# Second attention of a four-layer kernel: each score matmul one place later in TensorE's order, the fourth of a step behind the value products

## The reference, cut to what matters

```
def _L1_attn_ref(x, w_qkv, w_out, b_out):      # x: (4, 1024, 128), 16 heads of 8
    ...
    q, k = _apply_rope(q, cos_emb, sin_emb), _apply_rope(k, cos_emb, sin_emb)
    scores = jnp.einsum('bhqd,bhkd->bhqk', q, k) / jnp.sqrt(jnp.asarray(hd, x.dtype))
    attn = jax.nn.softmax(scores, axis=-1)
    out = jnp.einsum('bhqk,bhkd->bhqd', attn, v)
```

## Time and profile before

| what | value |
| --- | --- |
| median of 3 runs | 1924.15 us (1923.0 to 1927.66) |
| the profiled execution: its own time | 1922.64 us |
| its span, first to last instruction | 1920.8 us |
| PE / DVE / ACT busy over the span | 91% / 72% / 61% |
| second attention, first to last value product | 867.5 to 1565.9 us |

### The profile page before, as it was taken

The page is one execution under the profiler, slowest core; times in us unless marked ns, Lnnn a source line. Parts: engine busy times, 40 slices in busy tenths (PEclk is TensorE's granted clock), DMA queues, the critical chain, the costliest instruction groups (busy, mean ns, idle before and its releaser), DMA issues.

```text
span 1920.8 us, 31169 instructions
## 1 busy us (share of the span) xinstructions
PE 1743.9 (91%) x9328; PEld 844.8 (44%) x9328; DVE 1389.2 (72%) x2540; ACT 1162.8 (61%) x1801; POOL 97.0 (5%) x123
## 2 busy tenths in 40 slices
PE   6899999699999999579999999999999968988997
PEld 3334343366656656333333333333333325544553
DVE  3788888757777777478889888989898814455544
ACT  3888888544344444107777777777777754444443
POOL 1000000001111011010000000000000000011000
PEclk9899999889999999859999999999999988999999
DMA  7532121101111000210000000000100010000000
GB/s 220 140 92 60 49 62 47 66 1 34 33 33 33 29 10 28 66 41 22 22 23 21 22 21 21 22 22 21 37 26 21 2 44 1 6 6 11 5 5 11
DMA packets 44844, 68.99 MB, mean 36 GB/s; under 512 B 15952, under 2 KB 25056, under 8 KB 44144
## 3 DMA queue, kind: packets, MB, share of 16 engines
q1 hardware_dynamic: 44784, 68.28, 11.9%
HBM read 42.04 MB, written 26.21 MB: 36 GB/s over the span
## 4 chain that ended last, share of the span: by engine, by line
PE 70%; DVE 12%; ACT 9%; issue 5%; SPq 1%; DMA 1%; POOL 1%; DVEq 1%; ACTq 0%; POOLq 0%
PE full_o L689 13%; PE score L676 12%; PE hid_pair L960 11%; PE bank L1060 9%; ACT probs L738 6%; PE causal_o L451 5%; PE triple L435 4%; PE max_pair L652 3%; DVE cprobs L514 2%; PE bank L969 2%; PE bank L990 2%; DVE hid L1317 1%; PE bank L890 1%; PE max_pair L663 1%; DVE negmax L776 1%
## 5 line engine op out<-in xcount | busy, mean ns | idle before, releaser
L776 DVE TENSOR_REDUCE negmax<-max_pair 128x1 f32<-128x1024 f32 x512 | 599.9, 1218 | 69.4 <-PE max_pair L652 62.3
L738 ACT ACTIVATE probs<-score 128x512 f32<-128x512 f32 x1024 | 529.0, 603 | 150.8 <-PE score L676 150.8
L652 PE MATMUL max_pair<-k_st,q_st 64*128 64x512 f32 x1024 | 405.3, 474 | 22.2 <-DMA q_st<-q_scr 18.1
L676 PE MATMUL score<-q_st,k_st 64*128 64x512 f32 x1024 | 382.9, 451 | 34.0 <-ACT probs L738 24.6
L676 PEld LDWEIGHTS score<-q_st,k_st 64*128 64x128 f32 x1024 | 170.6, 185 | 304.7 <-ACT probs L738 284.9
L484 ACT ACTIVATE cprobs<-triple 128x1536 f32<-128x1536 f32 x192 | 268.5, 1456 | 38.5 <-PE triple L435 38.3
L689 PE MATMUL full_o<-probs,v_st 128*32 128x512 f32 x2048 | 272.9, 606 | 0.0
L960 PE MATMUL hid_pair<-x_hi,w_hi 128*128 128x512 f32 x384 | 206.8, 539 | 0.0
L652 PEld LDWEIGHTS max_pair<-k_st,q_st 64*128 64x128 f32 x1024 | 171.7, 191 | 79.5 <-DVE negmax L776 39.5
L1132 ACT ACTIVATE act_s<-hid_pair 128x512 f32<-128x512 f32 x128 | 76.4, 597 | 157.5 <-PE hid_pair L960 157.4
L514 DVE TENSOR_SCALAR cprobs<-cprobs 128x1536 f32<-128x1536 f32 (+6 forms) x272 | 163.0, 624 | 0.4 <-ACT cprobs L484 0.4
(11 more groups left out here) (129 smaller groups left out, 1594.0 us busy)
## 6 DMA issues: line engine op xcount, KB each, us to landing
k_st<-k_scr SPq DMA_DIRECT2D x64, 128.0 KB, 2.8
q_st<-q_scr SPq DMA_DIRECT2D x128, 64.0 KB, 2.3
q_st<-q_scr SPq DMA_DIRECT2D x16, 512.0 KB
k_st<-k_scr SPq DMA_DIRECT2D x64, 104.0 KB
q_scr<-qk_hi SPq DMA_DIRECT2D x24, 256.0 KB, 2.9
k_scr<-qk_hi SPq DMA_DIRECT2D x24, 256.0 KB, 3.1
q_scr<-qk_lo SPq DMA_DIRECT2D x16, 256.0 KB, 2.9
k_scr<-qk_lo SPq DMA_DIRECT2D x16, 256.0 KB, 3.2
```

Of the source, the lines that this page charges most:

```text
L652: ins = nc.tensor.matmul(ring[slot][:, half, :], q_st[p][rows, qt * P:(qt + 1) * P], k_st[p][rows, j, half * CH:(half + 1) * CH], start=Tr ...
L676: nc.tensor.matmul(sbank[L.score_bank(e)][:, :], k_st[p][rows, j, kt * P:(kt + 1) * P], q_st[p][rows, q0:q0 + w], start=True, stop=True, t ...
L738: nc.scalar.activation(probs[s % NP][:, j, :], sbank[L.score_bank(e)][:, :], ACT.Exp, scale=SCALE).then_inc(L.exp_done, 1)
L776: nc.vector.tensor_reduce(negmax[:, qt // TPC, j, qt % TPC:qt % TPC + 1], ring[slot][:, :, :].rearrange("p a n -> p (a n)"), AXX, ALU.max, ...
```

## The change

In every step the scores are issued one place later. Place 0 now holds the fourth score that the step before issued at its place 3, so that it stands behind the value products; places 1 to 3 hold the first three scores of step s + 2. The order of the heads within a step becomes 0, 2, 3, 1, by which each place keeps the half of the array that it had. ScalarE's Exp writes the matching slice of `probs`. Ahead of the first round 7 scores are issued where there were 8. Gap, banks, counts to wait for, the halves of the maxima, the value products, and the order on ScalarE, VectorE, SyncE and GpSimd stay.

```
+    HEADS = (0, 2, 3, 1)
...
-            s, j = e // HG, e % HG
+            s, j = e // HG, L.HEADS[e % HG]
             qc, kt, q0, w, _ = L.steps[s]
-            if j == 0 and kt == 0:
+            if e % HG == 0 and kt == 0:
                 pe.wait_ge(L.aug_loaded[p][qc], 16 * 2 * (i // 2 + 1))
...
-                to = s + AHEAD
-                ahead = (i, p, to) if to < L.S else (i + 1, 1 - p, to - L.S) if nxt else None
                 pairs = L.pairs_at(s, nxt)
                 for j in range(HG):
-                    if ahead:
-                        pe_score(pe, L, ahead[0], ahead[1], HG * ahead[2] + j)
+                    e = HG * (s + AHEAD) + j - 1
+                    if e < L.E:
+                        pe_score(pe, L, i, p, e)
+                    elif nxt:
+                        pe_score(pe, L, i + 1, 1 - p, e - L.E)
...
-            for e in range(HG * AHEAD):
+            for e in range(HG * AHEAD - 1):
                 pe_score(pe, L, 0, 0, e)
...
-                nc.scalar.activation(probs[s % NP][:, j, :], sbank[L.score_bank(e)][:, :], ACT.Exp,
+                nc.scalar.activation(probs[s % NP][:, L.HEADS[j], :], sbank[L.score_bank(e)][:, :], ACT.Exp,
```

## The result

| | before | with the change |
| --- | --- | --- |
| median of 20 runs | 1919.85 us | 1927.47 us |
| ratio, 95% interval | | 1.0036 (1.0022 to 1.0049) |
| the profiled execution: its own time | 1922.64 us | 1932.16 us |
| its span | 1920.8 us | 1930.3 us |
| second attention, start of the first value product to start of the last | 697.8 us | 703.6 us |

By the ratio the change costs 6.9 us (4.2 to 9.4); the two medians themselves lie 7.6 apart. The forecast was +2.4 us, and its range, 1920 to 1932, held the time. Ratios here are of fast runs alone; the one run that this leaves out anywhere took 3805 us, one of ten of the version with half 0 first, and no profile shows why. The profile's 9.5 us is more than the change's share: the second attention accounts for 5.8 of them.

A forecast was written before the change was run, and what follows sets the result against it. A loop over TensorE and ScalarE, 2.61 us a step through three score banks, was taken as the bound. Terms +7.1 - 2.9 - 1.7 - 0.1 = +2.4 us on a median of 1924.15 gave 1926.6 us, range 1920 to 1932.

The forecast's parts named there:

- Interior step: Usual steps of the second attention: the loop of scores, Exps and value products stays at 2.61 us, a change of 0.
- The rival of a broken loop: Interior steps: place 3 no longer waits, steps fall towards VectorE's 2.35 us, about -60 us, near 1865; chance 0.05.
- Steps 8 and 0: Steps with the output save: ScalarE's copy leaves the loop, 0.10 us won in each of 29 steps, -2.9 us.
- Static rounds: Rounds 0 and 15: the Exp on the path has one wait fewer, 0.06 us less in 28 steps, -1.7 us.
- Steps 6 and 14: Left-out bank: place 2 stalls for the Exp of place 0, 0.23 us in each of 31 steps, +7.1 us.
- place 3 follows at once: Steps 6 and 14: score 34 starts 0.34 us behind the stalled place 2, value products another 0.32 later.
- upper bound of 0.34: Steps 6 and 14: cost per stall if value products follow the second pair by the full 0.43, 10.5 us in all.
- Start and tail: Before the first value products one score fewer, -0.5 us; at the end the last score comes later, +0.3 to +0.4.
- SyncE: Loads of the stacks of round i + 2 are issued 1.4 us later, covered by 8 us, so no cost.
- Within 0.3%: Whole-kernel time differing by less than 0.3% (5.8 us), about what a measurement can't tell from none; chance 0.71.
- slower: Whole kernel slower by over 0.3%: dear stall, half of the longer Exp and the forecast's upper edge; chance 0.21.
- The dear-stall rival: Steps 6 and 14 lose 0.34 us each and the save at steps 8 and 0 wins nothing, +8.8, 1933 us; chance 0.16.

The follow-up runs named there:

- the version with half 0 first: Changed kernel with half 0 of pair b's maxima issued ahead of the score at place 2 in steps 6 and 14; ratio 1.0019 to the kernel before.
- the copy put back: Changed kernel with the earlier turn, plus ScalarE's output copy again ahead of the Exp of place 0; 1918.44 us, ratio 0.9987 to the kernel before.
- the exchanged waits: Kernel before, with the two waits of a step's first Exp exchanged in static rounds 0 and 15 (score first, then value products); ratio 1.0005.
- the earlier turn: Changed kernel with the left-out bank turn one score earlier, ahead of scores 31 and 63; 1915.19 us, ratio 0.9974 to the kernel before.
- the first experiment: The changed kernel unaltered, measured and profiled again beside the kernel before on one chip; ratio 1.0033.

## Why the prediction was right, and where it was short

- **Interior step, 0.** Right: 2.61 in every step between the breaks. The loop runs over three banks, and renaming its members leaves it as it is. The rival of a broken loop is out.
- **Steps 8 and 0, -2.9.** Right: 2.67, forecast 2.68, against 2.78; the copy put back restores 2.78.
- **Static rounds, -1.7.** Right: 2.61, against 2.67; the exchanged waits give the same in the old order. The two static steps 8 had been put at nearly nothing and are 2.76 for 2.70, 0.1 us in all. One static step stands apart: step 14 of round 0 took 2.95 before, its Exp 0.88 behind place 0; with the change it is 2.84, and 2.61 with the earlier turn. Where its extra 0.28 came from is not shown; it lowers the difference of the profiles by as much and stands in no term of the sum.
- **Steps 6 and 14, +7.1.** The place and the stall were right; this is the term that was sized too small. The step was "place 3 follows at once", which took the half of the maxima at place 2 to start with its score. In the 28 looped cases it starts 0.08 later, so each costs 0.31 and not 0.23: 28 x 0.31 + 3 x 0.23 = 9.4, 2.2 more than forecast. My upper bound of 0.34 held it.
- **Start and tail.** 0.55 won at the start (from the first score to the first value product 7.91 us for 8.46), 0.56 lost at the end; forecast were -0.5 and +0.3 to +0.4.
- **SyncE.** Right: no wait of TensorE for the stacks appeared.
- **The sum.** With the corrected term it is +9.4 - 3.1 - 1.7 + 0 = +4.6. From first score to last value product the two profiles of the changed kernel show +5.3, of which 0.8 is the clock in step 1, and +4.4. The ratio's interval, 4.2 to 9.4 us, holds 4.6; its middle is 2 us higher. The runs of the first experiment narrow this down. Among runs of one kernel there (31 before, 12 with the change), a run is about 1.4 us longer for each 0.001 that its mean granted clock is lower, and the changed kernel's runs had 0.0005 less on average. At an equal clock the two kernels are 5.0 us apart there, an estimate with a standard error of 0.3. For the first comparison the clocks of the runs before are not on record, so its 2 us stay open.
- **The time.** That the forecast median of 1926.6 lies only 0.9 from the measured 1927.47 is luck. It stood on a median of 3 runs, 1924.15; over 20 runs the kernel before has 1919.85. Of the difference the forecast had 2.4 us where 6.9 were measured. Carried over as a difference, the range was -4 to +8, and it still holds the 6.9, near its upper end.
- **The side.** "Within 0.3%" had 0.71 and "slower" 0.21; the measured ratio lies just beyond 0.3%, with an interval on both sides of it. The dear-stall rival was nearer on one half (it had 0.34 a stall, the looped ones took 0.31) and wrong on the other (the save did win).

## What to carry to other kernels

A rotation of buffers that leaves out a turn, to come out even at a loop's end, is a part of the schedule: the two scores behind it wait for a more recent Exp than the others do, and here this was free only where the value products stood between them, or where the two scores used different rows of the array. Whoever moves the order by one place should look at the turn with it; here, on one chip, moving it turns +0.33% into -0.26%. And an operation outside the loop on the path, like the copy, was better placed behind that loop's member in its engine's queue: it gave 0.11 us a step.

## What the runs showed of the hardware that was not expected

- A matmul with a wait count from a register, behind a stalled matmul, started 0.08 to 0.09 later than its neighbour in other rows of the array (977.80 for 977.71 above); with a constant count, in round 0, both started at 889.44.
- Matmuls in different halves of the array did not always start in program order; "each engine takes its queue in order", said at the start, is too strong for TensorE's starts. With the heads in order 0, 1, 2, 3 the half beside place 0's score wants the same rows as that score. The program has score, half, score, half; the timeline of TensorE has both scores first, and the first half 0.34 behind:

```profile
977.86 0.54 PE L677 MATMUL score<-q_st,k_st 64*128 64x512 f32 x2
978.20 0.62 PE L653 MATMUL max_pair<-k_st,q_st 64*128 64x512 f32 x2
```

The same shows in the kernel with half 0 first: half 1, written behind score 34, starts at 967.50, 0.33 ahead of it.
